# Convolution of a graph network on one core: handing the shared row on with one 128x128 product instead of four on 32-column tiles

## What is computed

```python
h = silu(edge_scalars @ fc_w1 * (1 / sqrt(8))) * SILU_NORM
w_a, w_b, w_c, w_d = split(h @ fc_w2 * (1 / sqrt(64)), 4)      # per edge, 64 each
xg0, xg1 = y0[edge_src], y1[edge_src]                           # gathered rows
mids = concat([w_a*xg0*ea0, w_b*sum(xg1*ea1), (w_c*xg0)[:, :, None]*ea1[:, None],
               (w_d*ea0)[:, :, None]*xg1])
agg = segment_sum(mids, edge_dst, num_segments=n)               # sum per destination
...
x = layernorm(x + convolution(x))
x = layernorm(x + attention(x))
```

## Time and profile before

| | |
|---|---|
| time, median of 3 runs (4498.87 to 4500.8) | 4499.56 us |
| span of the profiled execution | 5824.1 us |
| TensorE passes, busy over the span | 4650.5 us (80%) |
| VectorE busy | 3605.8 us (62%) |
| GpSimd busy | 3218.0 us (55%) |
| ScalarE busy | 1536.9 us (26%) |
| gathers of the convolution, first to last start | 86.9 to 2890.3 us |
| gathers of the attention, first to last start | 2950.3 to 5745.2 us |

### The profile page before, as it was taken

How to read it: one execution, slowest core, us unless ns; L and a number is a source line. 1 busy time by engine, 2 the same in 40 slices (tenths; PEclk the granted TensorE clock), 3 DMA queues, 4 the chain that set the end, 5 groups by cost and what they waited for, 6 DMA issues and landing times. The chain is left out here.

```text
span 5824.1 us, 116189 instructions
## 1 busy us (share of the span) xinstructions
PE 4650.5 (80%) x33992; PEld 2943.9 (51%) x33992; DVE 3605.8 (62%) x10598; ACT 1536.9 (26%) x3203; POOL 3218.0 (55%) x3385
## 2 busy tenths in 40 slices
PE   6888888888888888888847777777777777777777
PEld 4444444444444444444435665555556555565555
DVE  3566666666666666666526666666666666666666
ACT  3121222212222222222213333333333333333333
POOL 3555555555555555555445555555555555555552
PEclk8999999999999999999967777777777777777777
DMA  6444444444444444444433333333333333333331
GB/s 228 126 127 122 132 125 127 129 123 135 122 130 127 125 132 122 130 126 124 135 94 95 90 93 94 93 92 91 94 92 91 94 93 93 93 92 94 95 92 52
DMA packets 410283, 649.87 MB, mean 112 GB/s; under 512 B 138008, under 2 KB 270442, under 8 KB 410204
## 3 DMA queue, kind: packets, MB, share of 16 engines
q0 software_dynamic: 161120, 444.76, 27.5%
q1 hardware_dynamic: 249084, 204.19, 11.6%
HBM read 546.95 MB, written 101.68 MB: 111 GB/s over the span
## 5 line engine op out<-in xcount | busy, mean ns | idle before, releaser
L977 POOL DMA_INDIRECT sub_xg<-y_rows,sub_meta x1668 | 1599.1, 959 | 1208.1 <-PE sub_a L1027 558.7
L2342 POOL DMA_INDIRECT ord_xg<-xpa_rows,ord_meta x1666 | 1597.6, 959 | 1201.8 <-PE ord_a L2410 548.0
L2410 PE MATMUL ord_a<-ord_xg,ord_sel 128*128 128x264 f32 x3332 | 1330.0, 542 | 91.5 <-DVE ord_xg L2773 66.5
L1027 PE MATMUL sub_a<-sub_mids,sub_sel 128*32 128x128 f32 (+1 forms) x13344 | 1119.7, 312 | 311.8 <-issue 215.3
L2410 PEld LDWEIGHTS ord_a<-ord_xg,ord_sel 128*128 128x128 f32 x3332 | 834.9, 275 | 255.8 <-DVE ord_xg L2773 76.1
L1347 DVE TENSOR_TENSOR sub_mids<-sub_w,sub_xg 128x256 f32<-128x256 f32 x834 | 351.1, 421 | 983.7 <-remote 790.2
L1027 PEld LDWEIGHTS sub_a<-sub_mids,sub_sel 128*32 128x32 f32 x13344 | 463.0, 110 | 810.8 <-issue 545.8
L1352 DVE TENSOR_TENSOR sub_mids<-sub_w,sub_xg 128x384 f32<-128x384 f32 x1668 | 844.4, 548 | 0.0
L2358 PE MATMUL ord_s<-ident,ord_sel 128*128 128x128 f32 x1666 | 348.2, 337 | 569.7 <-ACT ord_sel_t L2476 539.6
L1007 PE MATMUL sub_w<-sub_fc,sub_ht 64*128 64x256 f32 x3336 | 611.8, 438 | 11.0 <-issue 10.7
L2358 PEld LDWEIGHTS ord_s<-ident,ord_sel 128*128 128x128 f32 x1666 | 244.3, 172 | 709.5 <-issue 684.5
(11 more groups left out here) (206 smaller groups left out, 4433.2 us busy)
## 6 DMA issues: line engine op xcount, KB each, us to landing
sub_sum_rows<-sub_agg_s SPq DMA_DIRECT2D x556, 64.0 KB
sub_node_rows<-sub_sum_rows SPq DMA_DIRECT2D x49, 640.0 KB, 5.6
sub_xg<-y_rows,sub_meta POOLq DMA_INDIRECT x1668
ord_xg<-xpa_rows,ord_meta POOLq DMA_INDIRECT x1666
ord_x_rows<-x_rows SPq DMA_DIRECT2D x119, 128.0 KB
out_dram<-ord_res SPq DMA_DIRECT2D x119, 128.0 KB
xpa_rows<-sub_proj SPq DMA_DIRECT2D x49, 264.0 KB, 2.2
lin_xt<-in_x_t_dram SPq DMA_DIRECT2D x14, 896.0 KB, 10.1
```

The costliest lines, as they stand in the source:

```text
L977: nc.gpsimd.indirect_dma_start(xg[:, b, k], None, y, bass.IndirectOffsetOnAxis(ids[:, b, 0, k:k + 1], 0))\
L1027: mm = nc.tensor.matmul(a[ROWS * m:ROWS * (m + 1), 0:w].rearrange("p (q f) -> p q f", f=MUL), sel[:, b, k, m], of, start=(j == 0), stop=False,
L2342: nc.gpsimd.indirect_dma_start(xg[:, b, k], None, xpa, bass.IndirectOffsetOnAxis(ids[:, b, k:k + 1], 0))\
L2410: mm = nc.tensor.matmul(psum_a[b % 2][:, 0:WIDE], sel[:, b, k], xg[:, b, k], start=(k == 0), stop=(k == TILES - 1 and not has(i, b, -1)), ...
```

## The change

The four products of `hand_on`, each with its strip of `hand_col` on a 32-column tile of the array, become one product with the whole 128 x 128 matrix, 256 columns wide. `hand_col` is zero outside the four columns it fills, and the columns 128 to 255 of strips 1 to 3 are zero in the banks, so the sums are the same.

```diff
                         before = agg_s[:, b if s > 0 else (b - 1) % SUB_TURN, (s - 1) % GROUP_SUBS]
-                        for m in (1, 2, 3, 0):
-                            part, w = slice(ROWS * m, ROWS * (m + 1)), 4 * MUL if m == 0 else 2 * MUL
-                            mm = nc.tensor.matmul(psum_a[s % 2][part, 0:w], hand_col[:, b, s, part], before[:, 0:w],
-                                                  start=False, stop=True, skip_group_check=True)
-                        mm.then_inc(summed, 1)
+                        nc.tensor.matmul(psum_a[s % 2][:, 0:4 * MUL], hand_col[:, b, s], before, start=False, stop=True,
+                                         skip_group_check=True).then_inc(summed, 1)
```

## The result

The changed kernel takes 4620.1 us (four runs, 4615.28 to 4621.19) against 4499.2: a ratio of 1.026, 95% interval 1.025 to 1.028, or 121 us more. The forecast was 4640 with a range of 4565 to 4670: the direction was right, and the rise was 121 us where 140 were forecast.

A forecast was written before the change was run, and what follows sets the result against it. The prediction took TensorE to bound the convolution, with GpSimd within 3%. Added hand-on cost of 148 us, less 8 us hidden in pauses from GpSimd, on 4499.6 gave 4640 us, range 4565 to 4670.

The forecast's parts named there:

- What bounds the kernel: Convolution loop: TensorE sets the pace at 2.60 us a pair of tiles, against GpSimd's floor of 2.52.
- The halts: First profile: 1325 us of its 5824.1 us span taken as the recorder's; work priced in stretches without a halt.
- The check against the median: 4500 less 2099 (attention gathers) and 226 (outside the gathers) leaves 2175 us, or 2230, for the convolution; TensorE's work is 2165.
- Price removed: Each hand-on on 32-column tiles: two passes of the 256-column fourth tile, 0.43 us; the other passes and loads cost nothing.
- price added: Each hand-on as two whole-array passes of 256 columns between other forms: 0.63 us.
- edges: Changes of array form around the hand-on: +0.20 us at a pair's end (278), +0.34 in its middle (277), 148 us unrounded.
- The room: TensorE's slack in the convolution, taken as pauses from GpSimd; 8 us of the added work allowed to hide there.
- the bound of 10 to 65 us: Convolution time that TensorE's 2165 us of work leave unfilled, by the check against the median.
- Partly hidden: Rival: GpSimd's gathers set the pace at 2.67 us a pair, TensorE pays only 85 us: 4585 us; chance 0.22.
- Free edge: Rival: changing between 128x32 tiles and whole array costs nothing, 0.43 us replace 0.43: 4500 us; chance 0.07.
- loads in a row: Rival: hand-on loads can't run under passes, so fewer loads gain 277 us: 4223 us; chance 0.03.
- The clock: Rival: extra edges drop TensorE to 1.2 GHz for 6% of the time, 139 us more: about 4780; chance 0.05 with dearer edges.

The follow-up runs named there:

- b_lead: The kernel before with LEAD 12 instead of 10, so GpSimd may gather twelve tiles ahead of the aggregation: 4503.2 us, ratio 0.999.
- b_dve: The kernel before with VectorE's edge placing moved to a turn's first four pairs and offsets made after the first product: 4470.6 us, ratio 0.992.

## Why the prediction came out as it did

*What bounds the kernel: right.* TensorE sets the pace of the convolution. The windows show it over the whole stretch this time (columns as in the earlier trace rows), first of the kernel before, then of the changed one:

```profile
200.00:2280.00 2080.00, 2036.57 (x22389) 1101.28 (x22389) 1650.30 (x4849) 567.49 (x1221) 1513.65 (x1574) 1.00 0.55 161
```
```profile
200.00:2400.00 2200.00, 2179.03 (x19258) 1043.10 (x19258) 1656.08 (x4852) 568.19 (x1223) 1508.01 (x1575) 1.00 0.52 153
```

Busy 97.9% before and 99.0% after. No wait for ScalarE's copies appears in the changed kernel either: its passes wait for VectorE alone in this window.

*The halts: right, as far as shown.* Another recording of the same kernel had none, and the prices read around them held.

*The check against the median: right.* The attention's gathers, put at 2099 us at least for GpSimd's pace, take 2102 (2470.2 to 4572.5 in the changed kernel). The convolution's gathers ran 2199.6 us in the kernel before and 2320.0 in the changed one, sources by line:

```profile
L977 POOL DMA_INDIRECT sub_xg<-y_rows,sub_meta x1668: 954/960/1252, 85.7 to 2285.3; - x186
```
```profile
L977 POOL DMA_INDIRECT sub_xg<-y_rows,sub_meta x1668: 951/957/1266, 86.1 to 2406.1; - x186
```

They differ by 120.4 us, while the two whole spans differ by 116.1: the change lies in the convolution alone, and the rest was some 4 us shorter in the second recording.

*Price removed, price added, edges: right.* 0.43 out, 0.63 in, 0.20 at the end and 0.34 in the middle of a pair; the earlier trace rows were enough, though no row had the edge from 128*32 to 128*128. The loader stood 0.41 us without loads before each L1042. The Trainium skill's rule in "TensorEngine Tiling (Array Packing)", Key Properties, that a change of the tiling mode drains TensorE, agrees with that at this edge too.

*The room: mis-sized, and put down to the wrong engine.* The term is "I allow 8 us: a pause that comes from GpSimd". It is some 25 (46 turns x 0.53), and VectorE's; with it 148 - 25 = 123 us are forecast and 118 to 121 measured. The wait that it hides in is 46 x 1.02 = 47 us, which the bound of 10 to 65 us had inside. What I didn't do is ask where in the turn TensorE waits, although the order of VectorE's work was there to read: the stretch of 9.20 us in which TensorE had no idle is a fifth of a turn and holds no end of one. In the recording with the halts this wait stood among many others of the same name; a turn would have had to be followed pair by pair.

*The rivals.* Partly hidden: the size lies between it and the forecast, but not by its mechanism, since the wait is VectorE's (b_lead, b_dve). Free edge, loads in a row: refuted by the 0.63 us and by 0.41 us of idle loader. The clock stayed at 1.00 from 200 us to the end of the windows above. One remark of the prediction was loosely worded: the 555 x 12 = 6660 fewer instructions in the page (116189 to 109529) are matmuls and loads, half each.

## What to carry to other kernels

A product that is small in one form isn't cheap in another. Between products on 32-column tiles, one on the whole array cost 0.20 us more where the form changed behind it anyway, and 0.34 where it cut the tiles' run in two, while four on tiles ride beside their neighbours. Here the price of an edge that no row showed could be taken from rows of other edges. Then follow one whole period of the loop, and find each wait in it. TensorE meets VectorE once in a turn here: work added before that point comes out of the wait, as long as there is some left, and work saved there goes into it and brings nothing.

## What was not expected of the hardware

A change of form costs less than its records suggest, and depends on the form. Past its two widest passes (2 x 0.216 us) the hand-on takes 0.20 us on 128 columns (0.63) and 0.15 on 64 (0.58), though the load record of 128 columns is 0.19 us long. It isn't simply proportional to the columns: one tile's four products on 32 columns take 0.57, which leaves 0.14. And a single recording of a program may be 29% longer than the next (5824.1 and 4503.2 us) while the undisturbed steps read in it have the same price: 1.43 us for a pair with a hand-on in both, 1.00 for one without.
